# A 512-step recurrence: six products of ones behind the gate products instead of two ahead of the scores, two GpSimd pieces moved, keys-on-partitions scores by single columns

## The reference

```
def step(h, x_t):
    score = einsum('bsh,bh->bs', enc_hiddens, h @ W)     # 77 keys, 4 batches
    attn = softmax(score)
    context = einsum('bs,bsh->bh', attn, enc_hiddens)
    gx = concat([x_t, context]) @ kernel + bias          # xz, xr, xh
    gh = h @ recurrent_kernel                            # hz, hr, hh
    z, r = sigmoid(xz + hz), sigmoid(xr + hr)
    h_new = z * h + (1 - z) * tanh(xh + r * hh)
```

## Time and profile before

| what | us |
|---|---|
| median of 3 runs (3037.65, 3051.28, 3051.21) | 3051.21 |
| the profiled execution's own time | 3035.75 |
| its span | 3033.6 |
| recurrence: from the first state, 999.9, to the last, 2918.3 | 1918.4 |
| busy in the span: PE, DVE, ACT, POOL | 2623.4, 1961.1, 1596.0, 999.8 |
| mean granted TensorE clock | 0.879 |

### The profile page before, as it was taken

The page is one execution under the profiler, slowest core; times in us unless marked ns, Lnnn a source line. Parts: engine busy times, 40 slices in busy tenths (PEclk is TensorE's granted clock), DMA queues, the critical chain, the costliest instruction groups (busy, mean ns, idle before and its releaser), DMA issues. The chain is left out here.

```text
span 3033.6 us, 137372 instructions
## 1 busy us (share of the span) xinstructions
PE 2623.4 (86%) x57249; PEld 1752.5 (58%) x57250; DVE 1961.1 (65%) x7220; ACT 1596.0 (53%) x5266; POOL 999.8 (33%) x1992
## 2 busy tenths in 40 slices
PE   7999999888778899898999898999889777777769
PEld 4666666575455465565565565666556444444449
DVE  5666666774442677677777687777768555665553
ACT  4666666533443566576666575666567332222222
POOL 2000000131010467355677355666445110000016
PEclk9999999999878899799999899999989775555569
DMA  4000000000011100011000010000000000000013
GB/s 144 5 5 5 7 5 5 12 1 0 16 34 35 53 14 16 11 34 36 26 16 14 13 41 25 23 14 11 7 20 26 18 6 6 5 5 6 5 43 84
DMA packets 51914, 64.75 MB, mean 21 GB/s; under 512 B 7447, under 2 KB 36580, under 8 KB 51172
## 3 DMA queue, kind: packets, MB, share of 16 engines
q1 hardware_dynamic: 47204, 50.33, 5.5%
q0 software_dynamic: 4096, 5.67, 0.9%
HBM read 46.38 MB, written 9.60 MB: 18 GB/s over the span
## 5 line engine op out<-in xcount | busy, mean ns | idle before, releaser
L2267 POOL TENSOR_TENSOR gru_terms<-gru_states,gru_signs 128x8 f32<-128x8 f32 x512 | 104.2, 203 | 810.6 <-DVE gru_states L2551 693.0
L2188 ACT ACTIVATE gru_p_t<-gru_ps_tc,gru_negmax 128x12 f32<-128x12 f32 x512 | 138.8, 271 | 374.3 <-DVE gru_negmax L2520 207.0
L1755 PE MATMUL gru_ps_tc<-ctx_gate_w,gru_p_t 128*4 128x64 f32 x12288 | 314.5, 245 | 0.3 <-issue 0.2
L2191 ACT ACTIVATE gru_th_r<-gru_pre_r 128x32 f32<-128x32 f32 x512 | 118.6, 232 | 315.9 <-DVE gru_pre_r L2533 315.6
L2010 PE MATMUL gru_ps_sr<-score_w,gru_states 128*32 128x78 f32 x4096 | 196.8, 270 | 100.4 <-DVE gru_states L2551 99.2
L1755 PE MATMUL gru_ps_sr<-ctx_gate_w,gru_p_t 128*4 128x34 f32 x12288 | 211.3, 208 | 66.9 <-ACT gru_p_t L2188 65.9
L1755 PEld LDWEIGHTS gru_ps_sr<-ctx_gate_w,gru_p_t 128*4 128x4 f32 x12288 | 134.8, 91 | 229.2 <-ACT gru_p_t L2188 221.5
L371 ACT ACTIVATE self_probs<-self_sc,self_negmax 128x512 f32<-128x512 f32 x256 | 174.4, 685 | 167.4 <-DVE self_negmax L428 167.4
L2243 POOL TENSOR_SCALAR bg_probs<-bg_probs,bg_arsum 128x256 f32<-128x256 f32 (+2 forms) x192 | 242.2, 1261 | 19.0
L2021 PE MATMUL gru_ps_ox<-late,gru_states 128*4 128x128 f32 x4096 | 244.6, 308 | 1.4 <-ACT late L2123 1.4
L1755 PEld LDWEIGHTS gru_ps_tc<-ctx_gate_w,gru_p_t 128*4 128x4 f32 x12288 | 222.3, 97 | 0.8 <-issue 0.7
(11 more groups left out here) (420 smaller groups left out, 6606.4 us busy)
## 6 DMA issues: line engine op xcount, KB each, us to landing
bg_w<-in_moe_w SPq DMA_DIRECT2D x48, 256.0 KB, 2.9
bg_wa<-in_wqkv SPq DMA_DIRECT2D x24, 192.0 KB, 2.4
moe_w<-in_moe_w SPq DMA_DIRECT2D x16, 256.0 KB, 3.4
best_w_sb<-in_ec_w SPq DMA_DIRECT2D x16, 256.0 KB, 3.4
x_products<-late SPq DMA_DIRECT2D x16, 240.0 KB, 2.4
late<-x_products SPq DMA_DIRECT2D x240, 16.0 KB
cross_scratch<-ctab_raw SPq DMA_DIRECT2D x16, 154.0 KB
cross_outs<-cross_scratch POOLq DMA_DIRECT2D x4, 576.0 KB, 6.2
```

The costliest lines, as they stand in the source:

```text
L1755: last = pe.matmul(bank[32 * c:32 * c + B, 0:hi - lo], p_t[:, B * k:B * k + B], gate_w[:, k, GATE_ALL * c + lo:GATE_ALL * c + hi], start=k ...
L2188: act.activation(p_t[:], ps_t, ACT.Exp, bias=negmax[:, 0:1]).then_inc(s_exp, 1)
L2191: act.activation(th_r[:, 1:64:2], pre_r[:], ACT.Tanh, scale=0.5).then_inc(s_thr, 1)
```

## The change

- Two products of ones ahead of the scores become six, right behind the gate products of the step before and whatever `after_gates` put there, into another bank (`ps_ox`); they wait for DVE's reading of that bank (`s_own`), not for `precz`. Step 0 has none.
- Turning rows, the gating's three pieces, turning the history and the choice's three pieces no longer count as background work, so such steps get the six as well.
- The mask product is gone. Each keys-on-partitions product moves one column of the state into one column of `ps_t`, the last chunk only for its 13 keys. The bank's first columns are set to -1e30 once, and what no product writes keeps that.
- `argument` (POOL) and `tangent` (ACT) of an expert chunk come one step later; the tangent now stands ahead of `unit_input`.
- POOL's scaling of the exponentials waits for the step's `c_in`.

```
-                for at, norm in norms_at(t, 4): ... turn_rows(at, norm); busy = True
+                ...                                 turn_rows(at, norm)
...
-                busy = t and after_gates(t - 1)
+                if t and not after_gates(t - 1):
+                    pe.wait_ge(s_own, t)
+                    for i in range(6):
+                        fill_in(2 * P, ps_ox)
...
                 wait_positive(pe, s_precz, t)
-                pe.matmul(ps_t, mask_l, mask_r, start=True, stop=False, skip_group_check=True)
-                if not busy:
-                    for i in range(2):
-                        fill_in(2 * P, ps_sr)
                 pe.wait_ge(s_h, t + 1)
...
-                        last = pe.matmul(ps_t[32 * b:32 * b + 32, B * k:B * k + B], score_w[:, b, 32 * k:32 * k + 32], state(t),
-                                         start=False, stop=True, ...)
+                        keys = min(32, CTX - 32 * k)
+                        last = pe.matmul(ps_t[32 * b:32 * b + keys, B * k + b:B * k + b + 1], score_w[:, b, 32 * k:32 * k + keys], state(t)[:, b:b + 1],
+                                         start=True, stop=True, ...)
...
             def after_candidate(t):
+                for g, n, m in chunks_at(t, 2):
+                    tangent(g, n, m)
                 for g, n, m in chunks_at(t, 0):
                     unit_input(g, n, m)
-                for g, n, m in chunks_at(t, 1):
-                    tangent(g, n, m)
...
                 row = probs[:, j, 0:(g + 1) * P]
+                pool.wait_ge(s_cin, t + 1)
                 pool.tensor_scalar(row, row, arsum[:, j:j + 1], None, ALU.mult).then_inc(s_apn, 1)
...
-                for g, n, m in chunks_at(t, 1):
+                for g, n, m in chunks_at(t, 2):
                     argument(g, n, m)
...
-            dve.memset(ps_tc[:], 0.0).then_inc(s_init, 1)
+            dve.memset(ps_tc[:, 0:P], -1e30)
+            dve.memset(ps_tc[:, P:BANK], 0.0).then_inc(s_init, 1)
```

More of the change, by code:

```diff
@@ L1948, in after_gates @@
                         turn_rows(at, norm)
-                        busy = True
                 for g, n, m in units_at(t, "project"):
@@ L2014, in _ @@
                     for b in range(B):
-                        last = pe.matmul(ps_t[32 * b:32 * b + 32, B * k:B * k + B], score_w[:, b, 32 * k:32 * k + 32], state(t),
-                                         start=False, stop=True, tile_position=(0, 32 * b), skip_group_check=True)
+                        keys = min(32, CTX - 32 * k)
+                        last = pe.matmul(ps_t[32 * b:32 * b + keys, B * k + b:B * k + b + 1], score_w[:, b, 32 * k:32 * k + keys], state(t)[:, b:b + 1],
+                                         start=True, stop=True, tile_position=(0, 32 * b), skip_group_check=True)
                 last.then_inc(s_turnedmm, 1)
@@ L2236, in qk_norms, with scale_probs @@
                 pool.tensor_tensor(rn[:], ss[:], power[:], ALU.pow).then_inc(s_rn, 1)
-            def scale_probs(g, n, m, j):
+            def scale_probs(t, g, n, m, j):
                 pool.wait_ge(s_aexp, 2 * m + j + 1)
@@ L2259, in after_history @@
                     for g, n, m in units_at(t, f"scale{j}"):
-                        scale_probs(g, n, m, j)
+                        scale_probs(t, g, n, m, j)
                 for at, norm in norms_at(t, 2):
```

## The result

| | before | after |
|---|---|---|
| median | 3049.80 us (4 runs, 3037.65 to 3051.28) | 2964.35 us (4 runs, 2956.79 to 2970.34) |
| profiled execution, its span | 3035.75, 3033.6 | 2956.79, 2955.0 |
| mean granted TensorE clock | 0.879 | 0.976 |

The changed kernel takes 0.9729 of the time of the kernel before (95% interval 0.9703 to 0.9756), some 83 us less by that ratio. The direction and the range held. 18 of them stand in the profiled execution already: of the 99 us that the sum had, it shows 79. The other 8 lie between it and the median.

What follows compares the result with a forecast made beforehand. The prediction saw a chain from state to state, with TensorE at half clock for 578.2 us of the recurrence. Terms -83 + 2 - 12 - 1 - 5 = -99 gave 2936.8 from 3035.75; plus 2, 2939 us, range 2905 to 2985.

Steps and rivals of the forecast that it cites:

- 1, six products, with their cost: Light steps of the recurrence: six products of ones hold the full clock, -83 us; choice and similar steps cost +2.
- 2, pieces of the experts: Expert steps: moved POOL and ACT work frees the state's scan, but PE is the next bound; -12 us.
- 3, scaling behind `c_in`: Attention steps: POOL's scaling no longer holds up the scan of `c_in`; tile 1 gains 3, tile 3 loses 2; -1 us.
- 4, mask product and columns: Steps where PE is late: dropping the mask product saves 0.11 to 0.12 in 50 steps, single columns 0; -5 us.
- 7 us for what would stay: Two steps left at half clock in each of six stretches, 0.61 us each.
- The first rival: Recurrence's end: the clock does not come up despite six products; 3018 us, chance 0.06.
- the one of a block in the way: Between gate products and scores: the six products delay the scores at half clock; 3136 us, chance 0.04.
- The +2 for such steps: Choice and a few like steps: scores wait for all six products; +2 us, bounds 0 to +15.
- The whole lock: Attention: POOL's scaling locks out DVE's state scan until the scaling ends; +107 us, 3046 us, chance 0.03.
- The 0.54: Tile 3: a 512-column scaling on POOL blocks the state's scan only for its first 0.54 us.
- the loss of 0.08 per step: Tile 3: state's scan held 0.08 us by the scaling in 64 steps at most, half hidden by PE; +2 us.
- the 3.30 for the late steps: Late steps at the recurrence's end: 3.30 us each at full clock, against 3.91 at half clock.

Runs made afterwards that it cites:

- six alone: Kernel before with only the six products of ones behind the gate products, norms, gating, history and choice no longer background; 2947.11 us, ratio 0.9671.
- the kernel with one wait: Changed kernel, PE waiting ahead of the scores for the state alone: precz wait gone, own wait only where needed; 2935.66 us, ratio 0.9633.

## Why the prediction was right, and where it failed

| term | forecast | measured in the recurrence |
|---|---|---|
| 1, six products, with their cost | -83 + 2 = -81 | -89.3 (six alone: 1829.1 against 1918.4) |
| 2, pieces of the experts | -12 | -13.0 (1839.5 against 1852.5) |
| 3, scaling behind `c_in` | -1 | 0 (1839.5 against 1839.4) |
| 4, mask product and columns | -5 | -12.9 (1809.6 against 1822.5) |
| a wait on an instruction of its own | none | +26.5 (1839.5 against 1813.0) |
| sum | -99 | -89; the change itself -78.9 |

The terms were measured against different kernels: each beside its own neighbour, of which one profiled execution each is read. 10 us are left between their sum and the whole. A path of single changes adds up by construction and shows where they sit: the six alone -89.3; pieces moved, scaling behind `c_in` in tiles 1 and 2 and the wait for `own` dropped -6.6 (1822.5); mask product and columns out, with the wait for `precz`, -12.9 (1809.6); the wait for `c_in` in tile 3 as well +3.4 (1813.0); the two covered waits back +26.5 (1839.5). So the 10 us are in the second and third row of the table, which read -13.0 and 0 with the third wait in place, and -6.6 and +3.4 without it. How exact each number is, one execution can't tell: the same code outside the recurrence moved from 995.0 to 1003.6 us ahead of it and from 115.3 to 123.6 behind it over all these kernels.

That the sum came as near as it did is in part luck. A term of 26.5 us was missing, and the six products and the mask product gave 16 more than forecast, which made up for more than half of it.

**The clock.** Right in mechanism and nearly in size: the prediction counted 578.2 of the 597.5 us at half clock, and kept 7 us for what would stay. PE is busy 66% of the eight steps of the earlier trace rows and 66% (17.82 of 27.06 us) of eight late steps of the changed kernel, all at full clock; the forecast had 69%, as its step was shorter. The first rival fell with the clock line, the one of a block in the way with the 0.92 us between the sixth product and the scores. One part of it is real: in step 408 the six products stood right ahead of the scores, behind the choice's logits, and took 1.35 us at half clock. That step was 6.20 us long, and 6.71 before; in the other kernels with six it took 5.62 to 7.86. The +2 for such steps wasn't measured by itself.

**The expert steps.** Right in size beside the changed kernel (-12 against -13.0), where the third wait adds some 5 to it (13.2 against 7.9 in the expert phases), so that the agreement is in part luck. The scan is at 0.18 and the scores come right behind the product down, as forecast. The steps are of 3.69, not about 3.6: PE wasn't the last of the bounds. DVE's hidden units wait for the same product and then stand ahead of the maximum. The row for it was in the trace before, and the prediction followed the chain only as far as the scores. With the units behind the maximum the steps are 3.60.

**The scaling.** The whole lock is refuted: the state's scan goes through 1.03 us before the scaling ends. The 0.54 was right, the loss of 0.08 per step was 0.15, as POOL starts 0.17 behind `c_in`. So the wait costs 5.6 us in tile 3 where +2 was forecast (386.6 against 381.0), and gives 4.0 in tile 1 where 3 was. By the Trainium skill, SBUF — State Buffer, section "SBUF: two separate sides", the pair of ports is locked for the whole GpSimd instruction; the trace shows a lock at its start and not to its end.

**The step that failed** is a sentence of part 4, that "nothing in fewer moved columns can lose", and the 3.30 for the late steps that rested on it. It priced the mask product as 0.11 us of PE. The mask product was also what two of the three waits stood ahead of. With it gone, all three came together at the first score product, and the state's, which came late in 353 of the 512 steps of the kernel with one wait, went to an instruction of its own: +0.08 us per step, 26.5 us in all. The term itself was mis-sized to the other side: 12.9 instead of 5, for mask product and columns together.

## What to carry to other kernels

When an instruction is removed, the waits that stood ahead of it move to the next one: with three together the late one was carried by a separate instruction here (+0.08 us per step, 0.9% of this kernel), so keep the late wait alone ahead of its matmul and drop waits that another one covers. Where an edit shortens one link of a chain, follow the chain to the next start of that link before naming the next bound. Here it went past the scores to what DVE did ahead of their maximum.

## What the runs showed of the hardware

- A weight load that carries its wait for the state itself starts 0.05 to 0.06 us behind the end of the scan. Behind a separate semaphore instruction (51 ns) it starts 0.12 behind it, and its matmul 0.03 later still. At half clock the price is the same (3.954 against 3.873 us).
- Four bf16 products of ones in a step hold the clock nearly as well as six here: clock mean 0.962 against 0.972, two don't (552 and 604 us of the recurrence at half clock, ahead and behind).
- A scan with two SBUF inputs on DVE that is held by a 512-column scaling on POOL is let go 0.54 us after the scaling's start, though that takes 1.57. With 384 columns it is 0.43 of 1.25, with 256 columns 0.32 of 0.93.
- Moving one column instead of four leaves the 24 keys-on-partitions products as long as they were (0.33 and 0.35 us). Their weight loads take 0.30 and 0.32, so the loads are the likely bound; no run shows that apart.
